# A recommendation tower on one core: two table lookups by product shrink to three tiles and the first tile's pair products move ahead of them

## The reference

```python
e = jnp.stack([tbl_0[ids[:, 0]], ..., tbl_26[ids[:, 26]]], axis=1)      # 512 x 27 x 128
interactions = jnp.einsum('bnd,bmd->bnm', e, e)
z = interactions[:, i, j]                                               # triu, k=1: 351 pairs
h = jnp.concatenate([z, dense_ctx], axis=1)                             # 367 columns
h = jnp.maximum(h @ W_top1 + b_top1, 0.0)                               # 512
h = jnp.maximum(h @ W_top2 + b_top2, 0.0)                               # 256
y = h @ W_top3                                                          # 1
```

## Time and profile before

| | before |
|---|---|
| device time, median of 3 runs | 110.33 us (110.22 to 110.46) |
| device time of the profiled execution | 109.96 us |
| span of its trace | 107.8 us |
| TensorE matmul busy | 99.6 us (92%), weight loads 84.2 us |
| DVE busy | 73.8 us (68%), ACT 70.4 us (65%) |
| GpSimd busy | 65.9 us (61%), of it 63.6 us in 61 gathers |
| DMA | 18.26 MB, mean 169 GB/s |
| granted TensorE clock | full in every slice |

### The profile page before, as it was taken

One profiled execution on the slowest core, in us unless ns is written; L12 is line 12 of the kernel. 1 busy time (PEld: TensorE's weight loads), 2 busy tenths in 40 slices (PEclk: granted clock), 3 DMA queues, 4 the chain that ended last, 5 costly groups with the idle time before them and its releaser, 6 DMA issues.

```text
span 107.8 us, 2420 instructions
## 1 busy us (share of the span) xinstructions
PE 99.6 (92%) x993; PEld 84.2 (78%) x993; DVE 73.8 (68%) x68; ACT 70.4 (65%) x100; POOL 65.9 (61%) x71
## 2 busy tenths in 40 slices
PE   4995999999999799999999879999999999997992
PEld 4993887777767687876778679999998897996790
DVE  3299999999999999999999943035245405622131
ACT  5039999999999999999999956144404241421021
POOL 3177788777787777787777787777777720005000
PEclk9999999999999999999999999999999999999999
DMA  1899688888869694869526412679653443034100
GB/s 42 192 365 340 167 301 292 207 257 300 223 250 250 193 305 135 239 207 222 177 49 204 185 49 55 213 131 253 222 93 78 150 128 53 9 132 81 24 0 1
DMA packets 13031, 18.26 MB, mean 169 GB/s; under 512 B 7601, under 2 KB 8446, under 8 KB 13020
## 3 DMA queue, kind: packets, MB, share of 16 engines
q1 hardware_dynamic: 9552, 12.90, 39.8%
q0 software_dynamic: 2016, 4.06, 13.8%
q10 hardware_dynamic: 1452, 1.14, 3.5%
HBM read 16.32 MB, written 1.77 MB: 168 GB/s over the span
## 4 chain that ended last, share of the span: by engine, by line
PE 43%; DVE 37%; issue 9%; DMA 8%; ACT 1%; SPq 0%; ACTq 0%; DVEq 0%
DVE hot L474 25%; PE psG L359 13%; DVE parts L479 10%; PE psG L340 8%; PE psG L386 5%; PE psH L402 5%; PE psT L318 4%; DMA pick_ids<-in_picked_ids 4%; PE psH L340 3%; PE psH L371 3%; DMA pair_grams<-gram 3%; DMA zT<-pair_grams 2%; PE psH L417 1%; DVE hot L460 1%; DVE hot L463 1%
## 5 line engine op out<-in xcount | busy, mean ns | idle before, releaser
L301 POOL DMA_INDIRECT rows<-in_tbl,ids_sb x61 | 63.6, 1042 | 21.7 <-issue 18.3
L340 PE MATMUL psG<-hot,parts 128*128 128x512 f32 x196 | 49.5, 401 | 2.4 <-ACT hot L564 1.2
L340 PEld LDWEIGHTS psG<-hot,parts 128*128 128x128 f32 x196 | 35.2, 188 | 13.5 <-DVE hot L474 4.8
L474 DVE TENSOR_TENSOR hot<-pick_ids,psH 128x1536 fp32r<-128x1536 int32 (+2 forms) x23 | 41.5, 1843 | 0.0
L560 ACT ACTIVATE hot<-pick_ids,row_no 128x512 fp32r<-128x512 int32 (+1 forms) x30 | 19.4, 710 | 0.0
L479 DVE TENSOR_TENSOR parts<-table,parts 128x1024 fp32r<-128x1024 f32 (+1 forms) x12 | 16.2, 1349 | 0.0
L564 ACT ACTIVATE hot<-hot 128x1024 fp32r<-128x1024 f32 (+2 forms) x12 | 15.0, 1247 | 0.4
L359 PEld LDWEIGHTS psG<-ET 128*54 128x54 f32 x512 | 13.3, 130 | 2.3 <-issue 1.6
L359 PE MATMUL psG<-ET 128*54 128x54 f32 x512 | 13.9, 213 | 1.3 <-issue 1.2
L487 DVE COPY gram<-psG 128x432 f32<-128x432 f32 x8 | 7.3, 911 | 10.8 <-PE psG L359 10.8
L571 ACT COPY gram<-psG 128x432 f32<-128x432 f32 x8 | 7.3, 914 | 11.2 <-PE psG L359 10.5
(11 more groups left out here) (31 smaller groups left out, 49.7 us busy)
## 6 DMA issues: line engine op xcount, KB each, us to landing
table<-in_tbl SPq DMA_DIRECT2D x6, 640.0 KB, 4.8
table<-in_tbl SPq DMA_DIRECT2D x6, 512.0 KB, 5.5
pick_ids<-in_picked_ids SPq DMA_DIRECT2D x11, 256.0 KB, 4.0
rows<-in_tbl,ids_sb POOLq DMA_INDIRECT x61, 3.8
pair_grams<-gram SPq DMA_DIRECT2D x4, 216.0 KB, 2.3
pair_grams<-gram ACTq DMA_DIRECT2D x4, 216.0 KB, 3.0
w_sb<-in_w SPq DMA_DIRECT2D x1, 768.0 KB, 4.4
w_sb<-in_w SPq DMA_DIRECT2D x1, 512.0 KB, 4.3
```

The costliest lines, as they stand in the source:

```text
L301: pool.indirect_dma_start(out=rows[:, n % RING, x, :], out_offset=None, in_=gathered_tables[f], in_offset=bass.IndirectOffsetOnAxis(ap=ids ...
L340: last = pe.matmul(picked_psum(k), parts[:, k % 2, x, c, :], hot[:, k % 2, c, looked_up(k)], start=x == 0 and c == 0, stop=x == 1 and c == ...
L474: dve.tensor_tensor(hot[:, k % 2, first:end, looked_up(k)], pick_ids[:, k % TABLES, looked_up(k)].unsqueeze(1).to_broadcast(shape), number ...
```

## The change

1. Two features instead of one (LATE = 2: k = 10 and k = 11) are gathered for the first tile and picked only for tiles 2 to 4. Both picks have 384 columns. The first tile then has 17 gathered features in five quads (4, 4, 4, 4, 1), the others four quads as before (4, 4, 4, 3): 17 quads and 62 gathers.
2. TensorE's loop ends with pick 9. The units of tile 0 come next, then pick 10, quad 9, pick 11, quads 10 and 11, units of tile 1, and layer 1 of tile 0 directly behind them. The one-hot and low part of k = 11 are made on DVE and ACT behind the copies of tile 0's units (step "prepare").
3. DUE is [1, ..., 9]: one quad behind each pick from 1 to 9.
4. split_low is two subtractions, of half the chunks each, for every k.
5. Gathers number 8, 11, 14, 17, 21, 24, 29, 33, 37, 42, 48, 51 wait for the end of picks 0 to 11, numbers 44, 45, 53, 54, 60 for units 0 to 4, and 57 and 59 for layers 1 and 2 of tile 0.
6. Layer 3 of tiles 0 to 2 takes the activations as its stationary operand and w3 as the moving one, so that its output is one column of 128 rows; these three tiles are written by a DMA of their own, the last one by another.
7. Fewer wait instructions in pick and layer 2; on ACT the last instruction of the one-hot (L564) of k = 10 and 11 comes behind the copy of the pick before.

```diff
-    FG = len(gathered_tables) - 1
+    FG = len(gathered_tables) - LATE
...
+    for t in range(T):
+        features = FG + (LATE if t == 0 else 0)
+        QUADS += [(t, list(range(f, min(f + 4, features)))) for f in range(0, features, 4)]
+        TILE_QUADS.append(len(QUADS))
...
-        return slice(P if k == FP - 1 else 0, B)
+        return slice(P if k >= FP - LATE else 0, B)
...
-    DUE = [2, 3, 4, 5, 6, 7, 9, 10, 10]
+    DUE = [1, 2, 3, 4, 5, 6, 7, 8, 9]
+    BEHIND_PICKS = [8, 11, 14, 17, 21, 24, 29, 33, 37, 42, 48, 51]
+    BEHIND_UNITS = [44, 45, 53, 54, 60]
+    BEHIND_LAYERS = [57, 59]
...
         def picked_psum(k):
 
-            return psH[:, 0, 0:T - 1, :].rearrange("p t s -> p (t s)") if k == FP - 1 else psG[:, k % 2, 0, :]
+            if k == FP - 2:
+                return psH[:, 0, 0:T - 1, :].rearrange("p t s -> p (t s)")
+            return psG[:, 0, 0, 0:B - P] if k == FP - 1 else psG[:, k % 2, 0, :]
...
-        steps = units(0) + [("write", 0), ("pick", FP - 1)] + quads(9, 10) + [("read", 0)] + units(1) + [("write", 1)]
-        steps += quads(10, 11) + [("layer1", 0)] + quads(11, 12) + [("layer2", 0), ("layer2_end", 0), ("unit", 2 * U), ("layer3", 0), ("unit", 2 * U + 1), ("write", 2)]
-        steps += quads(12, 13) + [("layer1", 1)] + quads(13, 14) + [("layer2", 1), ("layer2_end", 1)]
-        steps += quads(14, 16) + [("layer3", 1)] + units(3) + [("write", 3)]
+        steps = units(0) + [("write", 0), ("prepare", FP - 1), ("pick", FP - 2)] + quads(9, 10) + [("pick", FP - 1)]
+        steps += quads(10, 12) + [("read", 0)] + units(1) + [("write", 1), ("layer1", 0)] + quads(12, 13)
+        steps += [("layer2", 0), ("layer2_end", 0), ("unit", 2 * U), ("layer3", 0), ("unit", 2 * U + 1), ("write", 2)]
+        steps += quads(13, 14) + [("layer1", 1)] + quads(14, 15) + [("layer2", 1), ("layer2_end", 1)]
+        steps += quads(15, 17) + [("layer3", 1)] + units(3) + [("write", 3)]
...
                 if k >= TABLES:
-                    sp.wait_ge(low_ready, k - TABLES + 1)
+                    sp.wait_ge(low_ready, 2 * (k - TABLES + 1))
...
+            sp.wait_ge(y_ready, T - 1)
+            sp.dma_start(out[0:B - P, :].rearrange("(t p) o -> p (t o)", p=P), y_cols[:, :], allow_slow_non_contiguous=True).then_inc(out_done, 16)
             sp.wait_ge(y_ready, T)
-            sp.dma_start(out.rearrange("b o -> o b"), y_sb[:, :]).then_inc(out_done, 16)
+            sp.dma_start(out[B - P:B, :].rearrange("p o -> o p"), y_sb).then_inc(out_done, 16)
...
+                    if number in BEHIND_PICKS:
+                        pool.wait_ge(picked, BEHIND_PICKS.index(number) + 1)
+                    if number in BEHIND_UNITS:
+                        pool.wait_ge(multiplied[H - 1], 2 * (BEHIND_UNITS.index(number) + 1))
+                    if number == BEHIND_LAYERS[0]:
+                        pool.wait_ge(l1_done, N1)
+                    if number == BEHIND_LAYERS[1]:
+                        pool.wait_ge(l2_done, N2)
...
-                if k >= 2:
+                if k == FP - 1:
+                    pe.wait_ge(gram_dve, 1)
+                elif k >= 2:
                     pe.wait_ge(picked_out, k - 1)
...
-                    pe.wait_ge(picked_out, FP - 1)
+                    pe.wait_ge(picked_out, FP - LATE)
...
-                    last = pe.matmul(y_psum(t), w3_sb[:, k:k + 1], h2[:, k, :], start=k == 0, stop=k == N2 - 1)
+                    if t < T - 1:
+                        last = pe.matmul(y_psum(t), h2[:, k, :], w3_sb[:, k:k + 1], start=k == 0, stop=k == N2 - 1)
+                    else:
+                        last = pe.matmul(y_psum(t), w3_sb[:, k:k + 1], h2[:, k, :], start=k == 0, stop=k == N2 - 1)
...
-            for x in range(FP - 1):
+            for x in range(FP - LATE):
                 pick(x)
...
-                dve.tensor_tensor(parts[:, k % 2, 1, 0:CH[k], :], table[:, k % TABLES, 0:CH[k], :],
-                                  parts[:, k % 2, 0, 0:CH[k], :], ALU.subtract).then_inc(low_ready, 1)
+                half = CH[k] // 2
+                for first, end in ((0, half), (half, CH[k])):
+                    dve.tensor_tensor(parts[:, k % 2, 1, first:end, :], table[:, k % TABLES, first:end, :],
+                                      parts[:, k % 2, 0, first:end, :], ALU.subtract).then_inc(low_ready, 1)
...
-            for k in range(FP):
+            for k in range(FP - 1):
                 make_hot(k)
                 split_low(k)
...
-                if step == "unit":
+                if step == "prepare":
+                    make_hot(x)
+                    split_low(x)
+                elif step == "unit":
...
-            for x in range(FP - 1):
+            finish_last_hot(0)
+            for x in range(FP - LATE):
                 split_high(x + 1)
                 make_last_hot(x + 1)
+                if x + 1 < FP - LATE:
+                    finish_last_hot(x + 1)
                 pick_copy(x)
+                if x + 1 == FP - LATE:
+                    finish_last_hot(x + 1)
...
+            split_high(FP - 1)
             act.wait_ge(small_in, 48)
             for step, x in steps:
-                if step == "pick":
+                if step == "prepare":
+                    make_last_hot(x)
+                elif step == "pick":
                     pick_copy(x)
+                    if x + 1 < FP:
+                        finish_last_hot(x + 1)
```

More of the change, by code:

```diff
@@ L35, in dlrm_tower @@
     GH = G // H
-    QUADS = [list(range(f, min(f + 4, FG))) for f in range(0, FG, 4)]
+    QUADS = []
+    TILE_QUADS = []
+    for t in range(T):
+        features = FG + (LATE if t == 0 else 0)
+        QUADS += [(t, list(range(f, min(f + 4, features)))) for f in range(0, features, 4)]
+        TILE_QUADS.append(len(QUADS))
     NQ = len(QUADS)
-    def quad(t, q):
-        return QUADS[q] + [FG] if t == 0 and q == NQ - 1 else QUADS[q]
     def looked_up(k):
-        return slice(P if k == FP - 1 else 0, B)
+        return slice(P if k >= FP - LATE else 0, B)
     def how_many(k):
@@ L89, in sem @@
             return ctx.enter_context(nc.semaphore(name))
-        ids_sb = sb("ids_sb", [P, T, FG + 1], i32)
+        ids_sb = sb("ids_sb", [P, T, FG + LATE], i32)
         pick_ids = sb("pick_ids", [V, TABLES, B], i32)
@@ L109, in dlrm_tower @@
         h2 = sb("h2", [P, N2, P])
-        y_sb = table[0:1, 0, 0:B // D, :].rearrange("o a d -> o (a d)")
+        y_sb = table[0:1, 0, 0, 0:P]
+        y_cols = sb("y_cols", [P, T - 1])
         psT = pb("psT", [P, 2, 4, P])
@@ L143, in dlrm_tower @@
         dense_in = sem("dense_in")
-        gathered = [[sem(f"gathered_{t}_{q}") for q in range(NQ)] for t in range(T)]
+        gathered = [sem(f"gathered_{n}") for n in range(NQ)]
         first_ids_in = sem("first_ids_in")
@@ L198, in row_number @@
             return row_no[:, int(CH[k] != min(CH)), c:c + 1]
-        BY_DVE = [n >= DURING_PICKS and n % 2 == 0 for n in range(T * NQ)]
+        BY_DVE = [n >= DURING_PICKS and n % 2 == 0 for n in range(NQ)]
         def wait_copied(eng, n):
@@ L211, in quad_views @@
         def quad_views(n):
-            fs = quad(*divmod(n, NQ))
-            return (ET[:, n // NQ, :, fs[0]:fs[-1] + 1, :],
+            t, fs = QUADS[n]
+            return (ET[:, t, :, fs[0]:fs[-1] + 1, :],
                     psT[:, n % 2, 0:len(fs), :].rearrange("d f (s g) -> d g f s", s=S))
@@ L295, in _ @@
             pool.wait_ge(ids_in, 16)
-            for n in range(T * NQ):
-                t, q = divmod(n, NQ)
+            number = 0
+            for n in range(NQ):
+                t, fs = QUADS[n]
                 if n >= RING:
                     pool.wait_ge(filled, n - RING + 1)
-                for x, f in enumerate(quad(t, q)):
+                for x, f in enumerate(fs):
+                    if number in BEHIND_PICKS:
[6 more added lines that the diff above has]
+                        pool.wait_ge(l2_done, N2)
                     pool.indirect_dma_start(
@@ L303, in _ @@
                         in_offset=bass.IndirectOffsetOnAxis(ap=ids_sb[:, t, f:f + 1], axis=0),
-                    ).then_inc(gathered[t][q], 16)
+                    ).then_inc(gathered[n], 16)
+                    number += 1
             wait_written(pool, T - 1)
@@ L312, in transposes @@
             def transposes(n):
-                t, q = divmod(n, NQ)
-                pe.wait_ge(gathered[t][q], 16 * len(quad(t, q)))
+                fs = QUADS[n][1]
+                pe.wait_ge(gathered[n], 16 * len(fs))
                 if n >= 2:
                     wait_copied(pe, n - 1)
-                for x, f in enumerate(quad(t, q)):
+                for x, f in enumerate(fs):
                     last = pe.transpose(psT[:, n % 2, x, :], rows[:, n % RING, x, :], ident[:, :])
@@ L326, in pick @@
                         pe.wait_ge(first_half_ready, 1)
-                    else:
+                    elif x == 0:
                         pe.wait_ge(ready, k + 1)
```

(23 more changed lines are left out.)

4 lines of the change are left out of this document (2 added, 2 removed).

## The result

| | before | after |
|---|---|---|
| median of 20 runs each | 109.87 us | 110.74 us |
| ratio | | 1.0074, 95% interval 1.0045 to 1.0103 |
| profiled execution, its span | 109.96, 107.8 us | 111.11, 108.6 us |
| end of the compute chain (last DVE copy) | 106.25 us | 104.97 us |
| from there to the end of the span | 1.5 us | 3.6 us |

The time lies in the range, but the change went the other way than forecast.

The account below looks back on a forecast made before the run. DVE was taken to bound the kernel up to 51.4 us, then PE. Terms -5.65 + 3.67 + 0.69 = -1.29 from the profiled 109.96 gave 108.7, plus 0.37 for the median: 109.0 us, range 108.3 to 112.3.

Parts of the forecast that it names:

- Part 1: Unit 0 waits for pick 9, not pick 10, and starts at about 56.95 despite halved subtractions: gain 5.65 us.
- Part 2: PE's extra work before tile 1's units: 3.67 us for pick 10 and 0.69 for quads; unit 2 at 69.03.
- ACT was the tight one: ACT's queue ahead of the last one-hot chunks of k = 11 ends at 65.7, PE asks at 65.75: cost 0.
- Part 3: Layers of tiles 0 and 1: a net 0.24 us saved in PE's order, lost again waiting for tile 1's pairs.
- the pairs of tile 1 come sooner: At layer 1 of tile 1, PE runs on without waiting for pairs: -1.5 to -1.9 us, 108.5 us; chance 0.13.
- no change: Layer 3 in column form on PE: taken as 0.5 us for four matmuls, against 0.53 before.
- the last sentence on layer 3: First output DMA, issued at about 100, finishes before the last tile's at 106: cost 0.
- Part 4: Gathers and gates: met waits cost nothing; the last of 62 gathers starts at 84.9, lands before quad 16: cost 0.
- gathers hold DVE up: A gather getting in between subtraction halves delays the second by 0.94 us: +5.3 in all, 115.6 us; chance 0.04.
- the gathers are late: Gathers lose whole subtractions, the last starts at 88.7 and quad 16 waits: +1.9 us in all, 112.2; chance 0.17.

Follow-up runs that it names:

- f1_rows: The changed kernel with layer 3 and the output store as in the kernel before; 108.13 us against 109.89, ratio 0.9844.
- g4_quad9: f1_rows with quad 9's transposes moved into PE's 0.44 us of idle ahead of unit 0; 108.21 us, ratio 0.9882 to the kernel before.
- f5_whole: f1_rows with the subtraction in one piece again, nothing else; 111.24 us, ratio 1.0121 to the kernel before.

## Why the prediction was right and wrong

**Part 1, right.** A halved subtraction costs 0.07 more, against 0.06: 13.06 to 14.26 is 1.20 where the earlier trace rows had 1.13. Unit 0 starts at 57.31; the whole trace of this run began 0.33 later (first table cast 7.35 against 7.02), so 56.98 against 56.95 (56.2 + 0.60 + 0.09 is 56.89; the forecast's own terms were 0.06 short of it). f1_rows has 56.83, with the first cast at 6.85.

```profile
13.06 1.28 DVE L508 TENSOR_TENSOR parts<-table,parts 128x512 fp32r<-128x512 f32 x2
14.26 3.41 DVE L501 TENSOR_TENSOR hot<-pick_ids,psH 128x1536 fp32r<-128x1536 int32 x2
```

**Part 2, right.** Pick 10 takes 3.69 (3.67), the three quads 1.30 (1.32), unit 2 starts at 69.49 (68.98 in f1_rows, 69.03 forecast), 69.16 without the late start. ACT was the tight one, and is later by a hair: its last one-hot part ends just as PE asks for it,

```profile
64.86 1.17 ACT L598 ACTIVATE hot<-hot 128x1152 fp32r<-128x1152 f32 x1
```

64.86 + 1.17 = 66.03, and the chain breaks at 66.08. The term was put at 0, and g4_quad9 shows that nothing was left.

**Part 3, partly wrong, and so the match of the chain is in part luck.** The new idle in layer 1 of tile 0 is there (PE goes on at 73.90, 72.96 + 0.90 being ACT's copy), but it costs more: from the end of the units to the end of the layer 3.30 (72.88 to 76.18) against 2.75 before, 0.55 and not 0.35. And PE didn't wait for the pairs of tile 1: layer 1 follows quad 13 at once (82.31 + 0.59 = 82.90), and takes 2.68 where it took 2.92. SP's issue of the reads took 3.86 against 4.07. After, and then the two layers before:

```profile
73.90 2.27 PE psG L409 x18
...
80.03 0.54 PE psH L442 x4
...
88.61 0.57 DVE ET L481
```

```profile
74.32 2.75 PE psG L386 x24
...
84.01 2.92 PE psH L371 x24
```

| start of | before | after | shift | forecast | f1_rows, shift |
|---|---|---|---|---|---|
| unit 0 | 62.60 | 57.31 | -5.29 | -5.65 | 56.83, -5.77 |
| unit 2 | 70.32 | 69.49 | -0.83 | -1.29 | 68.98, -1.34 |
| layer 1 of tile 1 | 84.01 | 82.90 | -1.11 | -1.29 | 82.38, -1.63 |
| unit 6 | 90.54 | 89.22 | -1.32 | -1.29 | 88.70, -1.84 |

From unit 2 to unit 6 both new kernels gain 0.5 where the forecast had nothing: 0.23 of the wait, 0.24 of layer 1, and a little from quad 10. That is the rival "the pairs of tile 1 come sooner" (-1.5 to -1.9, chance 0.13), which did come for the chain. In the changed kernel a start that was 0.33 later hides it, so that -1.28 looks like the forecast. f1_rows, which has the new order without the new store, shows it: its median is 1.76 below the kernel before. Counted from the first table cast of each trace (f1_rows began 0.17 earlier than before), unit 6 starts 1.65 and 1.67 earlier in the two. Quad 16's copy on DVE, which now stands ahead of unit 6, costs nothing more: from the end of its transposes to unit 6 it is 0.63 (88.59 to 89.22), and before, with layer 3 in that place, 0.62. Layer 3 in column form takes 0.54 against 0.53; "no change" holds.

**The step that failed** is the last sentence on layer 3: "The first output DMA is issued when tile 2 is done, at about 100, and has until the last tile's at 106 to finish: 0." It was issued at 98.94 and done at 108.15. The store had no row and no bounds, though nothing in the trace before resembled a DMA of single 4-byte values. Its price is 2.0 us at the end of the kernel, above the gain of 1.28. It was no rival either, so the chance for slower (0.21) stood on other mechanisms, of which none came, and that 110.74 lies within 108.3 to 112.3 is luck: the upper part of the range was there for late gathers.

**Part 4, right.** Gathers are stretched to at most 1.60, the last one starts at 85.10 (84.9) and lands in time.

```profile
13.43 1.13 POOL L320 DMA_INDIRECT rows<-in_tbl,ids_sb  x1 [0.30 <-issue]
...
56.69 1.60 POOL L320 DMA_INDIRECT rows<-in_tbl,ids_sb  x1 [0.30 <-issue]
...
85.10 0.94 POOL L320 DMA_INDIRECT rows<-in_tbl,ids_sb  x1 [0.30 <-issue]
```

The gather of 13.43 began in the first half of a subtraction that ran from 13.06 in two halves of 0.60 each (start to start; each is printed as 0.68 long); 13.43 + 1.13 = 14.56, which is 0.90 behind the end of the first half at 13.66. It got in between the halves, and the second half wasn't late: the next one-hot starts at 14.26. So the rival by which gathers hold DVE up fell. The rule behind it (the Trainium skill, page "SBUF — State Buffer", section "Who interferes with whom": whichever issues first gets the shared port pair for the whole instruction, which is said there of DVE's 2-port modes and was carried over to this subtraction) is not what this trace shows for a gather: it waits for DVE's whole instruction, DVE doesn't wait for the gather's. f5_whole shows about what the rival "the gathers are late" would have cost: last start 87.6 (88.7 worked out, less the 0.6 that whole subtractions give back), 1.012 in place of 0.984.

## What to carry to other kernels

A kernel ends when its last output has landed, so a new output DMA needs a term of its own in the sum, with its row or with bounds, even when six microseconds of other work seem to cover it. Results kept one to a partition cost far more to store as single neighbouring 4-byte values than as one row or as pieces of 12 bytes, and such a store can hold up other transfers as well. When a milestone comes out as forecast, compare those ahead of it: here a late start and an unexpected gain cancelled. Cutting a DVE instruction in two can pay on another engine: 0.07 us each here, for 2.7 us net by way of GpSimd.

## What the runs showed that was not expected

- 128 or 384 single values of 4 bytes written side by side take 7.0 to 8.9 us from their issue when SP waits for them alone (0.4 issue, 6.6 to 8.5 wait), and 8.9 to 9.2 in the kernels that go on to the last tile's store; 384 of them 64 bytes apart take 3.3, 128 pieces of 12 bytes 2.2 to 2.8. The packets that the profile shows are over within some 2 us of the issue all the same.
- Behind a store of 128 such values a 216 KB write took 9.1 us to land (2.6 without) and a gather 8.8, though the gather comes from another queue: 11 us on the whole kernel when it is done three times. A row of 512 bytes beside such a store still took 1.1.
- A gather stalled by a subtraction in two pieces goes on at the end of the first, 0.9 us before its own end, and the second piece isn't delayed.
- Gathers that start in the picks land later than those of the tail: in f5_whole 4.8 us after their start (median, 5 to 30 us) and 3.8 (30 to 60 us), against 2.6 to 3.4 for the tail's. Quad 3 was waited for 2.8 us there, and 0.5 in the changed kernel, where DVE's chain hides it.
